# Recurrent attention on one core: its 32 steps as a straight program instead of a loop

## What is computed

```
def attend(h):
    q = h @ Wq.T
    alpha = softmax(einsum('bc,bsc->bs', q, context))        # 512 keys for each sequence
    ctx = einsum('bs,bsc->bc', alpha, context)
    return tanh(concatenate([ctx, h]) @ Wout.T + b_out)

def step(carry, x_t):
    h, c, attn = carry
    gates = concatenate([x_t, attn]) @ W_ih.T + b_ih + h @ W_hh.T + b_hh
    i, f, g, o = split(gates, 4)
    c = sigmoid(f) * c + sigmoid(i) * tanh(g)
    h = sigmoid(o) * tanh(c)
    attn = attend(h)
    return (h, c, attn), attn
_, outs = scan(step, init, x over its 32 tokens)
```

## Time and profile before

| | us |
|---|---|
| median of 3 runs | 694.99 |
| lowest, highest | 694.54, 697.08 |
| the profiled execution, its own time | 696.79 |
| its span, first to last instruction of the program | 695.0 |
| the recurrent layer, from its first output tanh to the last | 236.74 to 473.90 |

### The profile page before, as it was taken

How to read it: one execution, slowest core, us unless ns; L and a number is a source line. 1 busy time by engine, 2 the same in 40 slices (tenths; PEclk the granted TensorE clock), 3 DMA queues, 4 the chain that set the end, 5 groups by cost and what they waited for, 6 DMA issues and landing times.

```text
span 695.0 us, 21604 instructions
## 1 busy us (share of the span) xinstructions
PE 569.2 (82%) x8469; PEld 440.0 (63%) x8469; DVE 480.8 (69%) x1894; ACT 298.3 (43%) x851; POOL 163.3 (23%) x209
## 2 busy tenths in 40 slices
PE   3958768577996689999998999996688988898857
PEld 2625544255884588888888888885366656665535
DVE  1567828965444677777777777773589898989882
ACT  2857825135555433323323233332454555554501
POOL 3234543108000000000000000000653466336600
PEclk9969989798998555555555555555899999999995
DMA  8800000001002000000000000000000000000000
GB/s 339 367 1 1 1 4 1 2 11 33 1 1 91 3 3 0 0 0 0 0 0 0 0 0 0 0 0 1 0 1 1 0 2 1 0 1 1 0 1 8
DMA packets 6056, 15.26 MB, mean 22 GB/s; under 512 B 2640, under 2 KB 3288, under 8 KB 5504
## 3 DMA queue, kind: packets, MB, share of 16 engines
q1 hardware_dynamic: 5296, 11.19, 4.4%
q10 hardware_dynamic: 720, 3.55, 1.3%
HBM read 14.60 MB, written 0.13 MB: 21 GB/s over the span
## 4 chain that ended last, share of the span: by engine, by line
PE 37%; DVE 33%; ACT 14%; issue 11%; POOL 2%; DMA 1%; DVEq 1%; SPq 0%; ACTq 0%; POOLq 0%
PE bank L1688 7%; PE bank L1597 6%; PE bank L1756 5%; ACT esp L678 3%; PE bank L1548 2%; DVE ssum L1144 2%; ACT a L664 2%; ACT e L680 2%; PE bank L1535 2%; DVE rz L1181 2%; DVE zs L1179 2%; DVE asp L1134 2%; DVE opre L1120 2%; DVE w L1201 2%; DVE esp L1163 1%
## 5 line engine op out<-in xcount | busy, mean ns | idle before, releaser
L474 POOL MEMSET ctxT<- 128x128 f32 x1 | 0.3, 316 | 303.9 <-DVE xres L1188 303.9
L1597 PE MATMUL bank<-esp,qblk 128*128 128x1 f16 (+1 forms) x2048 | 66.6, 166 | 0.7 <-ACT esp L678 0.7
L1597 PE MATMUL bank<-hsp,kT 128*128 128x2 f16 x2048 | 63.6, 166 | 2.2 <-DVE hsp L1172 1.7
L664 ACT ACTIVATE a<-opre 128x4 f32<-128x4 f32 x64 | 13.1, 205 | 115.3 <-DVE opre L1132 115.3
L1597 PEld LDWEIGHTS bank<-esp,qblk 128*128 128x128 f16 x2048 | 61.3, 104 | 1.2 <-ACT esp L678 1.1
L1597 PEld LDWEIGHTS bank<-hsp,kT 128*128 128x128 f16 x2048 | 60.0, 104 | 3.1 <-DVE hsp L1169 1.7
L1214 DVE SCALAR_TENSOR_TENSOR T<-bank,bct,T 128x256 f32<-128x256 f32 x112 | 46.4, 473 | 2.2 <-PE bank L1769 2.2
L1597 PE MATMUL bank<-asp,lsp 128*128 128x4 f16 x768 | 30.7, 168 | 16.3 <-DVE asp L1134 16.3
L1597 PEld LDWEIGHTS bank<-asp,lsp 128*128 128x128 f16 x768 | 25.4, 105 | 27.8 <-DVE asp L1134 27.7
L1201 DVE TENSOR_TENSOR_SCAN qblk<-ctxT,bank 128x512 f32<-128x512 f32 x32 | 37.7, 1207 | 5.7 <-PE bank L1756 5.3
L1201 DVE TENSOR_TENSOR_SCAN w<-kT,bank 128x512 f32<-128x512 f32 x32 | 37.5, 1205 | 1.1 <-PE bank L1756 1.1
(11 more groups left out here) (327 smaller groups left out, 1399.2 us busy)
## 6 DMA issues: line engine op xcount, KB each, us to landing
w<-in_w_dram SPq DMA_DIRECT2D x2, 2048.0 KB
ctxT<-in_ctxT_dram SPq DMA_DIRECT2D x8, 256.0 KB, 13.5
wqkv<-in_qkvT_dram ACTq DMA_DIRECT2D x1, 1536.0 KB, 12.0
w<-in_mw_dram SPq DMA_DIRECT2D x1, 1024.0 KB, 5.2
lw<-in_lw_dram SPq DMA_DIRECT2D x1, 960.0 KB, 19.7
rows<-in_rows_dram ACTq DMA_DIRECT2D x1, 772.0 KB, 8.2
wqkv<-in_fw_dram SPq DMA_DIRECT2D x1, 532.0 KB, 3.5
T<-in_mask_dram ACTq DMA_DIRECT2D x1, 512.0 KB, 6.2
```

The lines of the kernel that those rows point to most:

```text
L664: act.activation(a32[:, g, :], opre[:, g, :], ACT.Tanh).then_inc(sem["at_32"], 1)
L1597: return pe.matmul(out, lhsT, rhs, start=start, stop=stop, skip_group_check=True)
```

## The change

`lstm_loop` is replaced by `lstm_steps`, in which Python writes all 32 steps out, on PE, DVE and ACT alike. Step numbers are constants then, and so are the values waited for and the addresses; `Steps` loses its base. No computing instruction is added, removed or moved against another on its engine.

```diff
     def sync(self):
-        self.eng.wait_ge(self.sem, self.base + self.n)
+        self.eng.wait_ge(self.sem, self.n)
...
-        def lstm_loop(engine, half, steps=None):
-            def turn(t):
+        def lstm_steps(half):
+            half(gates=(0, 0))
+            half(main=(0, 0), gates=(1, 0))
+            for t in range(S - 1):
                 half(main=(1, t), out=(0, t), gates=(0, t + 1))
                 half(main=(0, t + 1), out=(1, t), gates=(1, t + 1))
-            half(gates=(0, 0))
-            half(main=(0, 0), gates=(1, 0))
-            turn(0)
-            before = steps.n if steps else 0
-            with engine.Fori(0, (S - 2) // 2) as i:
-                if steps:
-                    steps.n, steps.base = 0, before + i * (2 * LSTM_STEPS)
-                turn(i * 2 + 1)
-                turn(i * 2 + 2)
...
             half(main=(1, S - 1), out=(0, S - 1))
             half(out=(1, S - 1))
...
-                    t = bass.ds(t, 1)
-                    act.activation(yT[:, g * BH:(g + 1) * BH, t].rearrange("p b t -> p (b t)"), opre[:, g, :], ACT.Tanh) \
+                    act.activation(yT[:, g * BH:(g + 1) * BH, t], opre[:, g, :], ACT.Tanh) \
...
-                    mm(bank[GATES[g]][:, 0:4 * BH], identb, gx[:, bass.ds(t, 1), k, :, g * BH:(g + 1) * BH], start=(k == 0))
+                    mm(bank[GATES[g]][:, 0:4 * BH], identb, gx[:, t, k, :, g * BH:(g + 1) * BH], start=(k == 0))
```

More of the change, by code:

```diff
@@ L113, in __init__ @@
     def __init__(self, eng, sem):
-        self.eng, self.sem, self.n, self.base = eng, sem, 0, 0
+        self.eng, self.sem, self.n = eng, sem, 0
     def __call__(self, ins):
@@ L302, in build @@
         SETUP = ML * MC * (MK + 1) + 3 + 6
-        LSTM_STEPS = 18
         L_ZEROED = 6
@@ L306, in build @@
         block = ctx.enter_context(nc.Block())
-        def lstm_loop(engine, half, steps=None):
-            def turn(t):
+        def lstm_steps(half):
+            half(gates=(0, 0))
+            half(main=(0, 0), gates=(1, 0))
+            for t in range(S - 1):
                 half(main=(1, t), out=(0, t), gates=(0, t + 1))
                 half(main=(0, t + 1), out=(1, t), gates=(1, t + 1))
-            half(gates=(0, 0))
-            half(main=(0, 0), gates=(1, 0))
-            turn(0)
-            before = steps.n if steps else 0
-            with engine.Fori(0, (S - 2) // 2) as i:
-                if steps:
-                    steps.n, steps.base = 0, before + i * (2 * LSTM_STEPS)
-                turn(i * 2 + 1)
-                turn(i * 2 + 2)
-            if steps:
-                assert steps.n == 2 * LSTM_STEPS
-                steps.n, steps.base = before + (S - 2) * LSTM_STEPS, 0
             half(main=(1, S - 1), out=(0, S - 1))
@@ L687, in _ @@
             act.wait_ge(sem["l_zero"], L_ZEROED)
-            lstm_loop(act, half)
+            lstm_steps(half)
             act.preload_act_table_set("natural_log_exp_and_others")
@@ L1185, in _ @@
                 dve.memset(t, x).then_inc(sem["m_setup"], 1)
-            lstm_loop(dve, half, step)
+            lstm_steps(half)
             dve.wait_ge(sem["y_tr"], 1)
@@ L1620, in output_gates @@
                 for (k, n), ready in zip(MEETS, ("at_hi", "at_hi", "at_lo")):
-                    if not (isinstance(t, int) and t == 0):
+                    if t:
                         pe.wait_ge(sem[ready], nth(g, t - 1))
@@ L1678, in _ @@
                 h_gates(g)
-            lstm_loop(pe, half)
+            lstm_steps(half)
             pe.wait_ge(sem["y_st"], 2 * S)
```

## The result

| | before | after |
|---|---|---|
| median (4 runs each) | 695.25 us | 683.1 us |
| lowest, highest | 694.54, 697.08 | 681.99, 684.05 |
| the profiled execution | 696.79 | 682.67 |
| its span | 695.0 | 680.9 |
| first to last output tanh of the recurrent layer | 237.17 | 225.03 |

The account below looks back on a forecast made before the run. The recurrent layer's chain was taken to pay for DVE's loop jumps and register operation: 8.6 (jumps) + 4.5 (plain halves) + 0.55 (entry, exit), in all 13.6 us, off 694.99 gives 681.4 us; range 678.5 to 686.5.

Parts of the forecast that it names:

- The straight half as the sample of all: Recurrent layer, straight code ahead of the loop: its one half of 3.55 us stands for every half after the change.
- 14 jumps, 8.6 us: Halves across the loop's jumps back: 4.16 us each on average would become 3.55, saving 8.6 us.
- 45 plain halves, 4.5 us: Halves inside loop bodies: 3.65 would become 3.55 us without DVE's register operation between cell and hidden state, saving 4.5 us.
- ACT's and PE's register operations, nothing: In the recurrent loop: removing these, and PE's jump, was priced at nothing beyond the intervals already counted.
- Fetching, nothing: Recurrent layer: about 50 more PE code packets, priced at zero between ends of 0 and 50 us; same argument for DVE and ACT.
- The sum in the layer: Recurrent layer: jumps, plain halves, loop entry and exit together save 13.6 us, or 230.17 - 61 x 3.55.
- Behind the layer, 2 us to either side: After the recurrent layer: only the start time changes, but clock level changes may move, allowed 2 us either way.
- From span to median: Whole kernel: profiled execution 1.8 us above the median, so 13.6 was taken from 694.99, giving 681.4 us.
- Starved PE: Rival, PE in the recurrent layer: packets fetched too late, the full 1.0 us each showing, 731 us; chance 0.04.
- only the jumps: Rival, recurrent layer: plain halves' 0.10 is not the register operation, 5.4 us comes back, 686.8 us; chance 0.02.
- a higher clock in the layer: Rival, recurrent layer: PE's clock rises from 1.2 to 2.4 GHz, at most 18 us more saved, 663 us; chance 0.03.
- The small part of each fetch that shows: Rival, recurrent layer: up to 0.1 us of each of 50 packets shows, 5 us, so 686.4 us; chance 0.04.

Follow-up runs that it names:

- DVE's loop kernel: Against the kernel before: PE and ACT written out, DVE alone left in its loop; median 695.98 us, ratio 1.0006.

## Why the prediction was right, and where it was off

Step by step:

- **The straight half as the sample of all.** Right. 58 intervals at 3.559. The prediction allowed for a rounding of 0.01 in its 3.55, 0.6 us over 61 halves; nearly all of that came, as the half is 3.559 and not 3.55: 61 x 0.0095 = 0.6 us less gain.
- **14 jumps, 8.6 us.** Right in sum. The gap of 0.55 on DVE is gone everywhere. The prediction read PE's overhead as costing nothing while DVE loops, and left its jump inside the 61 intervals. Both hold, but the jump isn't free: with DVE's gone and PE's kept, 0.12 show nearly each time, 1.5 us in all. The sum held because it was taken from intervals in which no engine has a loop, not from DVE's gap alone: 14 x 0.55 would have given only 7.7.
- **45 plain halves, 4.5 us.** Right at its place, `c2` to `hsp`, and nearly in size: the 45 halves average 3.647 before and lose 0.087 each, 3.9 us; the rest is the rounding of 3.55 again. The cause was named wrongly: not the number that DVE makes in a register but that the last wait to be fulfilled sat on another instruction than `hsp`. That has a practical side: it could be had in the loop, without writing out anything (689.12).
- **ACT's and PE's register operations, nothing.** Right: with DVE in its loop, their removal changed the layer by 0.02 us, and with DVE written out the plain halves are 3.56 with them too.
- **Fetching, nothing.** The step that failed, though its range covered it. On PE it was right: 43 packets in DVE's loop kernel without a longer half. On DVE it was not: of the ten passages to a new piece of 128 instructions in the layer, four showed, 0.08 + 0.16 + 0.30 + 0.35 = 0.9 us. The prediction said "the same argument holds for them"; but its sample, one straight half, is too short to hold a boundary of DVE, which comes every six halves, where PE's comes about every one. What it did give was the sign to look for, longer halves and gaps without a releaser.
- **The sum in the layer.** 13.6 less 0.6 less 0.9 is 12.1; measured 12.14. Nothing is left over.
- **Behind the layer, 2 us to either side.** 1.5 were gained there (221.1 to 219.6) and 0.45 ahead of it. Over all kernels here the stretch behind takes 219.6 to 222.4 us, with the same instructions, and the layer begins between 234.7 and 237.4: the stretch ahead varies as much, which the prediction did not allow for. Neither follows the length of the layer or the edit. The clock line differs there from kernel to kernel, as the prediction feared, but that it is the cause was not tested and stays open.
- **From span to median.** The profiled execution of before lay 1.5 above the median, that of after 0.4 below. The two spans differ by 14.1, the medians by 12.15. So the agreement of the medians' difference with the layer's 12.14 is partly chance; the layer's number is the sound one. Of the 1.7 us between the forecast 681.4 and the median 683.1, 0.26 are before's median with its fourth run (695.25 for 694.99), and 1.45 are 13.6 less the medians' 12.15, which is close to the layer's 12.14 by that chance.
- **The rivals.** Starved PE, only the jumps, a higher clock in the layer: none came. The small part of each fetch that shows is true in kind, on DVE instead of PE, at a fifth of the price it was given (0.9 instead of 5).

## What to carry to other kernels

Find a ruler on the chain, an instruction that comes once in each step, and compare its distances at the ends and in the middle of a loop: if a straight piece exists anywhere, it prices the unrolled program including what is late next, which a sum of gaps on one engine does not. A short piece does not hold everything: here DVE's passages to new code come only every six halves. Put the wait that is fulfilled last on the instruction that needs it (here: write it first), and keep register counts off that spot, before unrolling anything. Time a half unrolled body before trusting it: the one of 12 halves, no longer held, was the worst of the three here, 9.5 us slower than the one of four.

## What the runs showed of the hardware

- A jump back cost DVE 0.55 us and PE 0.2 when the body was held, and both over 3 us when it was not; 4 halves of this kernel were held on PE and DVE, 12 were not.
- Where the last wait ahead of `hsp` stood apart from it, it cost 0.07 us a half; on a register operation, 0.09.
- DVE's straight code came in pieces of 128 instructions. Four of ten passages from one to the next cost 0.07 to 0.37 us, the others nothing; 43 packets for PE left no sign.
- Fetching this straight program on three engines took 4 GB/s in the layer.
